# A fused four-layer network on one core: the mixture layer's loads and shared expert rearranged, and softmax sums inverted as rows in two of its attentions

## The chip, the core and the metric

The program runs as one launch on 1 core of one Trainium2 chip. The metric is the device time of that launch in microseconds (us). TensorE multiplies matrices; VectorE (DVE), ScalarE (ACT) and GpSimd (POOL) work on elements; SyncE (SP) issues most DMAs.

## What is computed

Four layers are applied to `x` (32 sequences of 56 tokens, 128 features). Each adds a gated attention over a context of 1500 keys per sequence, and then a gated feed-forward part. Cut to what matters here:

```python
# layer 1 and layer 3 attention (16 heads of 8 features; layer 3 adds -1e6 * mask, and biases)
attn = softmax(einsum('bqhd,bkhd->bhqk', q, k) * scale, axis=-1)
out = einsum('bhqk,bkhd->bqhd', attn, v).reshape(B, T_q, 128)
return out @ w_o.T

# layer 1 feed-forward: one shared expert, 8 experts, each token goes to its best two
def _swiglu(x, gate_up, down):
    g, u = split(einsum('bsd,fd->bsf', x, gate_up), 2, axis=-1)   # 938 hidden
    return einsum('bsi,di->bsd', silu(g) * u, down)
out = _swiglu(x, shared_gate_up, shared_down)
for e in range(8):
    out = out + cw[..., e:e + 1] * _swiglu(x, experts_gate_up[e], experts_down[e])
```

Layers 0 (masked attention) and 2 (cosine attention and a small mixture) are not touched by the change.

## The kernel before, in words

The parts run one after the other, each in a block of its own that ends with a barrier of all engines: attention 0, feed-forward 0, attention 1, mixture layer 1 (`sort_tokens`, then `ffn1`), attention 2, feed-forward 2, attention 3, feed-forward 3, with a `norm` ahead of each.

**`turned_attention`** is attention 1 ("plain") and attention 3 ("add", with a mask). The outer loop goes over the 32 sequences n, the inner over the 8 head pairs p. TensorE's order is written out by hand: for each p `score` half 0, `turn` third 0, `score` half 1, `turn` third 1, `side_work`, `turn` third 2. `score` makes 112 x 750 logits in PSUM, DVE's `shifted` copies them and takes the maxima, DVE or ACT subtracts these (`lower`), `turn` transposes them two pairs later, ACT's `exp` takes them out, and `weigh` (p = 6, 7 and, of the next sequence, 2, 3) multiplies by the values. `side_work` is: the keys of sequence n + 2 (p = 0 to 2), its values (p = 3 to 5), and the end of sequence n - 1 (p = 6 and 7). All side work shares one PSUM tile, `side`.

The end of a sequence is a chain over three engines. ACT's `mix` copies the weighted values to `mixed` (p = 4). At p = 6 TensorE's `sums` multiplies them by `tile_sum`, a 128 x 128 matrix, so that each of 128 rows holds the softmax sum of its head; DVE's `invert` takes the reciprocal of 128 x 224 numbers. At p = 7 DVE's `normalise` multiplies, TensorE's `out` (4 matmuls with the output matrix) waits for it, and ACT's `finish` copies the result out when p = 0 of the next sequence begins.

**Mixture layer.** `sort_tokens` routes the tokens and ranks them on DVE; its SP stream loads constants and the shared expert, writes zeros to `slots_in` in nine DMAs, and then issues the loads of the eight experts, an `up` (944 KB) and a `down` (472 KB, on 118 partitions) for each. `ffn1` then scatters each token's row to its two slots with 32 indirect DMAs on POOL, while TensorE runs the shared expert on 16 tiles of 112 tokens, each in two halves (8 matmuls of 112 columns up, 4 matmuls down); after it 35 blocks of 128 slots run through their experts in the same two halves, and POOL gathers the results. `up` of one half runs ahead of `down` of the half before; ACT's silu and DVE's multiply stand between them. The blocks need the sorted rows and all experts; SP loads the rows only when the scatters have landed.

Each f32 matmul shows as two passes in the trace, each with its own weight load; a transpose shows as one.

## Time and profile before

| | |
|---|---|
| median of 3 runs | 6507.41 us (6505.57 to 6512.12) |
| profiled execution, device time | 6505.09 us |
| its span, first to last instruction | 6503.3 us |
| TensorE busy | 5399.5 us (83%) |
| DVE busy | 4556.5 us (70%) |
| ACT busy | 3155.4 us (49%) |
| POOL busy | 1967.3 us (30%) |
| mean granted TensorE clock | 0.915 of full |
| attention 1 | about 1700 to 2847 us of the span |
| sort and mixture layer 1 | 2863 to 3319 us |
| attention 3 | about 5280 to 6388 us |

The span is the profiled execution's; 1.8 us of the device time lie outside it. The parts follow one another, so a stage's own end is what counts, and busy shares are only an average of stages with different limits.

### The profile page before, as it was taken

To read this page: it belongs to the slowest core of one execution; us is meant where nothing else is said; L and a number is where in the kernel's file an instruction comes from. 1 tells how busy PE (TensorE), PEld (TensorE's weight loads), DVE (VectorE), ACT (ScalarE), POOL (GpSimd) and SP (SyncE) were. 2 spreads that over 40 slices of the span, in tenths; PEclk is the share of its full clock that TensorE was granted. 3 is DMA by queue.
4 is the path that set the end of the run, shared out by engine and by line. 5 is a ranking of instruction groups with operands and counts; after the bars stand their busy time and mean duration, and the time that the engine had idled before them with its cause. 6 is when DMAs were issued, how large, how long until landed. Compare 5 with 4: busy or idle time off the path is not lost. (4 is left out here: it accounts for less than half of the span.)

```text
span 6503.3 us, 132525 instructions
## 1 busy us (share of the span) xinstructions
PE 5399.5 (83%) x51199; PEld 3938.7 (61%) x51199; DVE 4556.5 (70%) x9168; ACT 3155.4 (49%) x5932; POOL 1967.3 (30%) x1458
## 2 busy tenths in 40 slices
PE   2898898896599999955947999999999658888887
PEld 1777777775277777745933444444444437777775
DVE  6888888885177777751446777777777448778774
ACT  0666666664165555531224444444444225555552
POOL 4766766761122222201011111111110023333330
PEclk6999999998699999977978999999999769999998
DMA  4555555552366666631010000000000068888870
GB/s 109 124 121 125 122 121 125 122 120 54 75 120 131 133 129 126 132 87 50 23 27 25 15 19 14 14 19 14 14 19 4 5 128 148 143 150 150 146 138 10
DMA packets 368260, 544.58 MB, mean 84 GB/s; under 512 B 115654, under 2 KB 247880, under 8 KB 367390
## 3 DMA queue, kind: packets, MB, share of 16 engines
q1 hardware_dynamic: 365678, 533.44, 39.8%
q8 instruction: 378, 6.19, 0.5%
q0 software_dynamic: 2048, 3.67, 0.2%
q14 instruction: 156, 1.28, 0.1%
HBM read 413.08 MB, written 123.90 MB: 83 GB/s over the span
## 5 line engine op out<-in xcount | busy, mean ns | idle before, releaser
L635 DVE CUSTOM_DVE_ANT_0 attn_logits<-attn_scores,attn_shift 112x750 f32<-112x750 f32 x1024 | 943.5, 931 | 468.4 <-PE attn_scores L452 467.7
L555 ACT ACTIVATE attn_probs_t<-attn_pt 125x448 f32<-125x448 f32 x1536 | 831.2, 542 | 780.4 <-PE attn_pt L467 760.3
L467 PEld LDWEIGHTS attn_pt<-ident,attn_logits 112*125 112x125 f32 x6144 | 867.0, 191 | 222.3 <-issue 80.7
L467 PE MATMUL attn_pt<-ident,attn_logits 112*125 112x112 f32 x6144 | 926.2, 274 | 67.8 <-DVE attn_logits L649 42.1
L2241 PE MATMUL attn2k_pk<-attn_wk,attn2k_cn_t 128*125 128x512 f32 x1536 | 737.9, 602 | 39.5 <-ACT attn2k_cn_t L2312 36.7
L2252 PE MATMUL attn2k_pg<-attn2k_kn,attn2k_cn 125*128 125x512 f32 x1536 | 725.0, 594 | 4.5 <-ACT attn2k_gram L2320 2.3
L2407 DVE TENSOR_REDUCE attn2k_ss<-attn2k_sq 125x16 f32<-125x1024 f32 x384 | 467.0, 1216 | 255.4 <-ACT attn2k_sq L2349 255.3
L389 POOL CAST attn_k_parts<-xn_t 128x500 bf16<-128x500 f32 x192 | 199.4, 1039 | 1407.4 <-DVE xn_t L605 1407.3
L1141 ACT ACTIVATE attn_probs_t<-attn_pt 125x448 f32<-125x448 f32 x768 | 414.8, 540 | 308.5 <-PE attn_pt L1029 305.9
L2349 ACT ACTIVATE attn2k_sq<-attn2k_pk 125x1024 f32<-125x1024 f32 x384 | 391.9, 1021 | 326.3 <-PE attn2k_pk L2241 326.2
L452 PE MATMUL attn_scores<-attn_k_packed,attn_q_blocks 96*112 96x375 bf16 x2048 | 523.3, 338 | 24.6 <-POOL attn_q_blocks L379 17.9
L2241 PEld LDWEIGHTS attn2k_pk<-attn_wk,attn2k_cn_t 128*125 128x125 f32 x1536 | 274.1, 187 | 399.3 <-issue 296.9
L1017 PE MATMUL attn_scores<-attn_k_packed,attn_q_blocks 96*112 96x375 bf16 x1024 | 357.2, 349 | 149.3 <-DVE attn_tops L1310 149.3
L2419 DVE TENSOR_TENSOR attn2k_kn<-attn2k_pk,attn2k_rn 125x1024 f32<-125x1024 f32 x384 | 470.1, 1224 | 13.3
L2252 PEld LDWEIGHTS attn2k_pg<-attn2k_kn,attn2k_cn 125*128 125x128 f32 x1536 | 264.1, 192 | 298.2 <-issue 286.3
L1310 DVE CUSTOM_DVE_ANT_0 attn_logits<-attn_scores,attn_bias,attn_floor 112x750 f32<-112x750 f32 x342 | 337.9, 988 | 101.8 <-PE attn_scores L1019 100.2
L649 DVE TENSOR_SCALAR attn_logits<-attn_logits,attn_neg_top 112x1500 f32<-112x1500 f32 x320 | 375.5, 1173 | 0.1
L480 PE MATMUL attn_po<-attn_probs_t,attn_v 125*32 125x112 f32 x12288 | 371.7, 272 | 1.3 <-ACT attn_probs_t L555 1.3
L1130 ACT ACTIVATE attn_logits<-attn_logits,attn_neg_top 112x750 f32<-112x750 f32 x342 | 312.9, 916 | 113.7 <-DVE attn_neg_top L1318 111.6
L2223 POOL COPY attn2k_q_now<-attn_q_t 128x448 f32 (+1 forms) x32 | 17.8, 558 | 1135.4 <-PE attn2k_pz L2273 1135.4
L546 ACT ACTIVATE attn_logits<-attn_logits,attn_neg_top 112x750 f32<-112x750 f32 x384 | 351.2, 915 | 10.5 <-DVE attn_neg_top L643 8.8
L421 PE MATMUL attn_side<-attn_ctx_t,attn_wk 128*128 128x500 f32 x384 | 219.7, 655 | 152.8 <-DVE xn_t L605 86.1
(360 smaller groups left out, 10814.0 us busy)
## 6 DMA issues: line engine op xcount, KB each, us to landing
attn_k_packed<-k_scratch SPq DMA_DIRECT2D x384, 375.0 KB, 5.9
attn_k_packed<-k_scratch SPq DMA_DIRECT2D x384, 187.5 KB, 3.9
k_scratch<-attn_k_parts SPq DMA_DIRECT2D x64, 1125.0 KB, 7.4
attn_ctx_t<-in_ctx_t SPq DMA_DIRECT2D x64, 750.0 KB, 7.3
k_scratch<-attn_k_parts SPq DMA_DIRECT2D x96, 375.0 KB, 4.5
attn_ctx_t<-in_ctx_t SPq DMA_DIRECT2D x96, 250.0 KB, 4.6
attn2k_ctx<-in_ctx SPq DMA_DIRECT2D x32, 750.0 KB
attn_mask_in<-in_mask SPq DMA_DIRECT2D x192, 109.4 KB
```

The costliest lines, as they stand in the source:

```text
L452: last = pe.matmul(scores[h][0:PAIR, b, 0:QTR], q_blocks[:, n % 2, p, :, :].rearrange("p a s -> p (a s)"), k_packed[:, n % 2, p, h * HALF ...
L467: last = pe.transpose(pt[(3 * at + t) % 2][0:KC, (c % 4) * PAIR:(c % 4 + 1) * PAIR], logits[:, at % 3, c * KC:(c + 1) * KC], g.ident[0:PAI ...
L480: last = pe.matmul(po[32 * j:32 * j + 32, grp * PAIR:(grp + 1) * PAIR], v[:, n % 3, c, V1 * p:V1 * p + 32], probs_t[0:KC, grp, c, j * PAIR ...
L555: act.activation(probs_t[0:KC, p // 4, 4 * t:4 * t + 4, (p % 4) * PAIR:(p % 4 + 1) * PAIR], pt[(3 * at + t) % 2][0:KC, 0:QUAD].rearrange(" ...
L635: dve.tensor_tensor_reduce(out=logits[:, at % 3, cols].rearrange("p (b k) -> p b k", b=2), in0=scores[h][0:PAIR, :, 0:QTR], in1=shift[:, n ...
L649: dve.tensor_scalar(at, at, neg_top[:, n % 2, p:p + 1], None, ALU.add).then_inc(dve_lowered, 1)
L1141: act.activation(probs_t[0:KC, at % PV_RING, 4 * t:4 * t + 4, :], pt[(3 * at + t) % 2][0:KC, 0:QUAD].rearrange("p (c q) -> p c q", c=4), A ...
L2241: last = pe.matmul(pk[c % 2][0:KC, b, :], cn_t[:, c % 2, :], wk[:, b * HW:(b + 1) * HW], start=True, stop=True)
L2252: last = pe.matmul(pg[:, b, :], cn[:, j, c, :], kn[:, c % 2, b * HW:(b + 1) * HW], start=(c == 0), stop=(c == CH - 1))
L2349: act.activation(sq[:, c % 2, :].rearrange("p (a b) -> p a b", a=2), pk[c % 2][0:KC, :, :], ACT.Square).then_inc(sq_ready, 1)
L2407: dve.tensor_reduce(ss[:, c % 2, :], sq[:, c % 2, :].rearrange("p (h d) -> p h d", h=H2), AX.X, ALU.add).then_inc(ss_ready, 1)
L2419: dve.tensor_tensor(kn[:, c % 2, :].rearrange("p (h d) -> p h d", h=H2), pk[c % 2][0:KC, :, :].rearrange("p a (h d) -> p (a h) d", h=8), r ...
```

## The change

Attentions 1 and 3: `sums` makes the sums with `mixed` as the stationary operand, 112 rows by 8 head pairs, in two matmuls of 4 columns; `invert` takes the reciprocal of 112 x 8 numbers; a new `widen` on TensorE spreads them to 128 x 224 in `side` with eight matmuls of 32 weight columns and 112 moving columns; `normalise` reads `side`. `widen` takes the place of `out` at p = 7, and `out` goes to p = 0 of the next sequence, between `turn` 0 and `score` 1; `finish` follows the first `exp` of that p. `sums` waits for the `finish` of one sequence earlier than before.

Mixture layer: the down matrices are padded to 128 partitions (512 KB each); the expert loads leave the block of the sort and go to the head of `ffn1`'s SP stream; POOL, no longer the sort's SP stream, waits for the zeros. The shared expert runs on 4 quads of 448 tokens in 8 parts (2 matmuls of 448 columns up, 4 matmuls of 128 columns down into one PSUM bank), ACT copies a quad in one instruction. The blocks compute as before.

```diff
                 def sums(n):
                     pe.wait_ge(mixed_ready, n + 1)
                     pe.wait_ge(v_ready, 3 * min(n + 4, B))
-                    wait(pe, y_copied, n)
-                    pe.matmul(side[:, 0:2 * PAIR], tile_sum[:], mixed[:], start=True, stop=True).then_inc(sums_ready, 1)
+                    wait(pe, y_copied, n - 1)
+                    for grp in range(2):
+                        last = pe.matmul(side[0:PAIR, 4 * grp:4 * grp + 4], mixed[:, grp * PAIR:(grp + 1) * PAIR],
+                                         tile_sum[:, 0:128:32], start=True, stop=True)
+                    last.then_inc(sums_ready, 1)
+
+                def widen(n):
+
+                    pe.wait_ge(inv_ready, n + 1)
+                    for p in range(HP):
+                        last = pe.matmul(side[32 * (p % 4):32 * (p % 4) + 32, (p // 4) * PAIR:(p // 4 + 1) * PAIR],
+                                         inv[:, p:p + 1].broadcast_to((PAIR, 32)), g.ident[0:PAIR, 0:PAIR],
+                                         start=True, stop=True)
+                    last.then_inc(inv_wide, 1)
...
-                        sums(n - 1) if p == 6 else out(n - 1)
+                        sums(n - 1) if p == 6 else widen(n - 1)
...
                         if some:
                             turn(*before, 0)
+                        if p == 0 and n > 1:
+                            out(n - 2)
                         score(n, p, 1)
...
+                out(B - 2)
                 sums(B - 1)
+                widen(B - 1)
                 out(B - 1)
...
-                        if p == 0 and n > 1:
-                            finish(n - 2)
                         for t in range(3):
                             if before[0] >= 0:
                                 exp(*before, t)
+                            if p == 0 and t == 0 and n > 1:
+                                finish(n - 2)
...
-                finish(B - 2)
                 for p in (HP - 2, HP - 1):
                     for t in range(3):
                         exp(B - 1, p, t)
+                finish(B - 2)
                 mix(B - 1)
...
                 def invert(n):
                     dve.wait_ge(sums_ready, n + 1)
-                    dve.reciprocal(inv[:], side[:, 0:2 * PAIR]).then_inc(inv_ready, 1)
+                    wait(dve, inv_wide, n)
+                    dve.reciprocal(inv[:], side[0:PAIR, 0:HP]).then_inc(inv_ready, 1)
 
                 def normalise(n):
-                    dve.wait_ge(inv_ready, n + 1)
+                    dve.wait_ge(inv_wide, n + 1)
                     wait(dve, y_ready, n)
-                    dve.tensor_tensor(attn[:], mixed[:], inv[:], ALU.mult).then_inc(attn_ready, 1)
+                    dve.tensor_tensor(attn[:], mixed[:], side[:, 0:2 * PAIR], ALU.mult).then_inc(attn_ready, 1)
...
-                for e in range(E):
-                    sp.dma_start(o.up[:, e, :], a["experts_up_t"][e]).then_inc(o.experts_in, 16)
-                    sp.dma_start(o.down[:, e, :, :], a["experts_down_t"][e]).then_inc(o.experts_in, 16)
-                sp.wait_ge(o.slots_zeroed, 16 * ((NB + 3) // 4))
...
-        o.up, o.down = r.sb("up", [D, E + 1, 2 * FULL1]), r.sb("down", [F1C, E + 1, F1K, D])
+        o.up, o.down = r.sb("up", [D, E + 1, 2 * FULL1]), r.sb("down", [128, E + 1, F1K, D])
...
-        half = TILES
-        units = [("tile", t) for t in range(half)] + [("block", b) for b in range(NB)] + \
-            [("tile", t) for t in range(half, TILES)]
-        N = 2 * len(units)
+        units = [("quad", q) for q in range(NQ)] + [("block", b) for b in range(NB)]
+        parts = {"quad": F1K, "block": 2}
+        items = [(u, j) for u, (kind, n) in enumerate(units) for j in range(parts[kind])]
+        N = len(items)
...
+                for e in range(E):
+                    sp.dma_start(o.up[:, e, :], a["experts_up_t"][e]).then_inc(o.experts_in, 16)
+                    sp.dma_start(o.down[:, e, :, :], a["experts_down_t"][e]).then_inc(o.experts_in, 16)
                 load(0)
                 load(1)
...
             @block.gpsimd
             def _(pool):
+                pool.wait_ge(o.slots_zeroed, 16 * quads)
                 for t in range(TILES):
...
+                    if kind == "quad":
+                        wait(pe, h_ready, i - 1)
+                        for bank, at in ((pg, j * F1C), (pu, FULL1 + j * F1C)):
+                            last = pe.matmul(bank[i % 2][0:F1C, 0:QUAD], o.up[:, E, at:at + F1C],
+                                             g.xn_t[:, n * QUAD:(n + 1) * QUAD], start=True, stop=True)
+                        last.then_inc(up_ready, 1)
+                        return
...
+                        if kind == "quad":
+                            last = pe.matmul(py[u % 2][0:PAIR, k * D:(k + 1) * D], h[:, i % 2, k * PAIR:(k + 1) * PAIR],
+                                             o.down[0:F1C, E, j, :], start=(j == 0 and k == 0),
+                                             stop=(j == F1K - 1 and k == 3))
...
-    return np.ascontiguousarray(out.reshape(F1K, F1C, D).transpose(1, 0, 2))
+    return np.pad(out.reshape(F1K, F1C, D).transpose(1, 0, 2), ((0, 128 - F1C), (0, 0), (0, 0)))
```

## Rows read from the trace of the kernel before

**Rows 1.** Busy time by stretch: start:end, length, engines, PEclk, DMA share, GB/s.
```profile
2000.00:2400.00 400.00, 362.38 (x4323) 309.86 (x4323) 303.34 (x637) 235.00 (x421) 99.10 (x84) 0.96 0.69 131
5400.00:6500.00 1100.00, 931.98 (x10904) 780.64 (x10904) 819.83 (x1614) 583.86 (x1044) 353.52 (x218) 0.97 0.70 126
```

**Rows 2.** Order of time, TensorE, attention 1: start, us, what [idle before].
```profile
2102.89 0.56 PE L436 MATMUL attn_side<-attn_mixed,attn_tile_sum 128*128 128x224 f32 x2
2103.29 0.59 PE L467 MATMUL attn_pt<-ident,attn_logits 112*125 112x112 f32 x4
...
2106.21 0.59 PE L467 MATMUL attn_pt<-ident,attn_logits 112*125 112x112 f32 x4
2108.01 1.10 PE L441 MATMUL attn_side<-attn_attn,attn_wo 128*128 128x56 f32 x8 [1.21 <-DVE attn_attn L658]
2108.94 1.02 PE L467 MATMUL attn_pt<-ident,attn_logits 112*125 112x112 f32 x4
2109.89 2.47 PE L480 MATMUL attn_po<-attn_probs_t,attn_v 125*32 125x112 f32 x48
```

**Rows 3.** Order of time, TensorE, the same place in attention 3.
```profile
5904.47 1.10 PE L441 MATMUL attn_side<-attn_attn,attn_wo 128*128 128x56 f32 x8 [1.21 <-DVE attn_attn L658]
...
5905.98 1.36 PE L480 MATMUL attn_po<-attn_probs_t,attn_v 125*32 125x112 f32 x48
```

**Rows 4.** Order of time, DVE: the reciprocal, once a sequence, attentions 1 and 3.
```profile
2038.47 1.55 DVE L653 RECIPROCAL attn_inv<-attn_side 128x224 f32<-128x224 f32 x1
...
2072.17 1.55 DVE L653 RECIPROCAL attn_inv<-attn_side 128x224 f32<-128x224 f32 x1
...
2104.36 1.55 DVE L653 RECIPROCAL attn_inv<-attn_side 128x224 f32<-128x224 f32 x1
...
5866.80 1.54 DVE L653 RECIPROCAL attn_inv<-attn_side 128x224 f32<-128x224 f32 x1
...
5900.82 1.55 DVE L653 RECIPROCAL attn_inv<-attn_side 128x224 f32<-128x224 f32 x1
```

**Rows 5.** Order of time: a spread like the new one, a small reciprocal, ACT's finish.
```profile
678.14 0.92 PE L988 MATMUL attn_po<-ident,attn_share 112*32 112x112 f32 x16
...
2856.99 0.25 DVE L204 RECIPROCAL norm_rs<-norm_sd 112x16 f32<-112x16 f32 x1 [0.28 <-ACT norm_sd L215]
...
5906.53 0.30 ACT L566 ACTIVATE y_t<-attn_side,attn_bo 128x56 f32<-128x56 f32 x1
```

**Rows 6.** Order of time: the sort's last on DVE, then ffn1's first, and POOL's scatters.
```profile
2887.45 0.17 DVE L1863 TENSOR_SCALAR ffn_expert<-sort_expert 1x35 int32<-1x35 f32 x1
...
2961.78 0.71 PE L1972 MATMUL ffn_pg<-xn_t,ffn_up 128*118 128x112 f32 x2 [80.36 <-PEq L105]
...
2962.53 1.19 POOL L1927 DMA_INDIRECT slots_in<-rows,ffn_slot  x1 [98.74 <-POOLq L105]
...
3001.40 0.94 POOL L1927 DMA_INDIRECT slots_in<-rows,ffn_slot  x1 [0.30 <-issue]
```

**Rows 7.** SP's last expert load, and two 2 us stretches: clock, DMA share, GB/s.
```profile
2958.26 2.53 SPq L1778 DMA_DIRECT2D ffn_down<-in_experts_down_t  x1
...
2914.00:2916.00 2.00, 0.50 0.13 52
2936.00:2938.00 2.00, 0.50 0.97 373
```

**Rows 8.** Order of time, ACT and TensorE, during the scatters of ffn1.
```profile
3006.90 0.55 ACT L2026 ACTIVATE ffn_silu<-ffn_pg 118x448 f32<-118x448 f32 x1 [32.42 <-DMA q_scratch<-attn_probs_t]
...
3008.15 2.05 PE L1986 MATMUL ffn_py<-ffn_down,ffn_h 118*112 118x128 f32 x8 [19.12 <-DVE ffn_h L2047]
```

**Rows 9.** Order of time, TensorE: first block's transposes; a 500-column matmul and its successor.
```profile
3079.87 0.60 PE L1946 MATMUL ffn_pt<-ident,ffn_rows_in 128*128 128x128 f32 x4
...
2113.90 1.02 PE L421 MATMUL attn_side<-attn_ctx_t,attn_wk 128*128 128x500 f32 x2
2114.76 0.59 PE L467 MATMUL attn_pt<-ident,attn_logits 112*125 112x112 f32 x4
```

More of the change, by code:

```diff
@@ L1751, in sort_tokens @@
         ends, reached, expert = r.sb("ends", [1, E]), r.sb("reached", [1, NB, E]), r.sb("expert", [1, NB])
-        zeros = r.sb("zeros", [128, 4, D])
         pl = r.ps("pl", [128, TILES, E])
@@ L1918, in _ @@
                         load(b // 4 + 2)
-                    sp.wait_ge(taken, half + b + 1)
+                    sp.wait_ge(taken, NQ + b + 1)
                     sp.dma_start(slots_out[b * BLK:(b + 1) * BLK, :], rows_out[:, b % 4, :]).then_inc(
@@ L1970, in up @@
                         for bank, at in ((pg, 0), (pu, FULL1)):
-                            at += (4 * part + k) * F1C
-                            last = pe.matmul(bank[i % 2][0:F1C, k * w:(k + 1) * w], w_up[:, at:at + F1C], src,
+                            at += (4 * j + k) * F1C
+                            last = pe.matmul(bank[i % 2][0:F1C, k * BLK:(k + 1) * BLK], up_now[:, n % 2, at:at + F1C],
+                                             rows_t[:, n // 4 % 2, n % 4 * BLK:(n % 4 + 1) * BLK],
                                              start=True, stop=True)
@@ L2006, in take @@
                     kind, n = units[u]
-                    act.wait_ge(down_ready, 2 * u + 2)
-                    if kind == "tile":
-                        to = total[:, n, :]
+                    act.wait_ge(down_ready, done(u))
+                    if kind == "quad":
+                        act.activation(total[:, 4 * n:4 * n + 4, :].rearrange("p t d -> p (t d)"), py[u % 2][0:PAIR, :],
+                                       ACT.Copy).then_inc(taken, 1)
                     else:
                         wait(act, block_out[n % 4], 16 * (n // 4))
-                        to = rows_out[:, n % 4, :]
-                    act.activation(to, py[u % 2][0:width(u), 0:D], ACT.Copy).then_inc(taken, 1)
-                for i in range(N):
-                    u, part = divmod(i, 2)
+                        act.activation(rows_out[:, n % 4, :], py[u % 2][:, 0:D], ACT.Copy).then_inc(taken, 1)
+                for i, (u, j) in enumerate(items):
                     kind, n = units[u]
-                    if kind == "block" and part == 0:
+                    cols = cols_of(u)
+                    if kind == "block" and j == 0:
                         if n == 0:
@@ L2026, in _ @@
                     act.activation(silu[:, i % 2, 0:cols], pg[i % 2][0:F1C, 0:cols], ACT.Silu).then_inc(silu_ready, 1)
-                    if part == 1 and u:
+                    if j == 1 and u:
                         take(u - 1)
@@ L2039, in choose @@
                         :, bass.ds(e * (2 * FULL1), 2 * FULL1)]).then_inc(chosen_up, 1)
-                for i in range(N):
-                    cols = 4 * width(i // 2)
-                    if i == 2 * half:
+                for i, (u, j) in enumerate(items):
+                    kind, n = units[u]
+                    cols = cols_of(u)
+                    if u == NQ and j == 0:
                         choose(0)
@@ L2048, in _ @@
                                       ALU.mult).then_inc(h_ready, 1)
-                    if i % 2 == 0 and half <= i // 2 < half + NB - 1:
-                        choose(i // 2 - half + 1)
+                    if kind == "block" and j == 0 and n + 1 < NB:
+                        choose(n + 1)
                 dve.wait_ge(taken, len(units))
```

58 lines of the change are left out of this document (26 added, 32 removed).

## Prediction

> **What bounds the kernel now.** The parts run one after the other, so I read first the busy time by stretch, then, stage by stage, the instructions in order of time, and asked what each engine waits for at the place of the change. In the two attentions TensorE is busy 91% and 85% of the time, DVE 75%, ACT 59% and 53% [rows 1]. TensorE's order is written out by hand, so every bubble in it is paid in full, and there is one bubble per sequence at the change: `out` comes 1.21 us after the end of the `turn` before it and waits for `normalise` on DVE [rows 2, 3]. That chain is late because the reciprocal takes 1.55 us of DVE [rows 4]. In attention 1 the same place holds a second loss. The `turn` behind `out` takes 1.02 us instead of 0.59, and the `weigh` after it 2.47 instead of 1.36 [rows 2, 3]: TensorE's granted clock has fallen from 2.4 to 1.2 GHz right after the bubble. The distance from one reciprocal to the next shows this loss whole. It is 32.19 us from 2072.17 to 2104.36 and 33.70 us before [rows 4]; of the 28 distances in attention 1 ahead of the last two, 21 are the long ones. In attention 3 the plain distance is 34.02 us [rows 4] and only 2 of 27 are longer, by 1.6 us.
>
> In the mixture layer the sort's own work ends at 2887.45 + 0.17 us, but `ffn1` starts at 2961.78, and TensorE and POOL both stand idle until then [rows 6]. The block of the sort is held open by SP, which issues its last expert load at 2958.26 for 2.53 us [rows 7]: the issues are held back by the loads ahead of them. After that the shared expert is disturbed while POOL scatters: ACT starts a silu 32.42 us after its last work, TensorE then waits 19.12 us for the result of it, and both go on at 3007 to 3008, 4.6 us after POOL's last scatter ended (3001.40 + 0.94) [rows 6, 8]. From 3008.15 to the first block at 3079.87 TensorE runs without a gap [rows 8, 9], and so it does through the blocks, which compute as before.
>
> **The change, part 1: attentions 1 and 3.** For one sequence, on TensorE:
> - `sums` before: 0.40 us (2102.89 to 2103.29) [rows 2]. After: four passes that each load 112 weight columns for 4 moving columns. Nearest row: `out`, eight passes bound by their weight loads, takes 0.93 us from its start to the next (2108.01 to 2108.94) [rows 2], so 0.116 a pass, 0.46 us in all. It costs 0.06.
> - `widen`, new: sixteen passes of 32 weight columns by 112. The same form in attention 0 took 0.92 us [rows 5]; `weigh`, with the same shape in the same four column groups, takes 1.36 for 48 passes [rows 3], so 0.45 for 16. I take 0.45, since `weigh` runs at this very place; 0.92 is the upper end.
> - The bubble goes. In issue time it is 1.80 (2106.21 to 2108.01) less the 0.42 that a `turn` takes, 1.38 us [rows 2]. `normalise` is still wanted by `out`, but `out` now comes after a `turn`, a `weigh`, a `score` and another `turn`, some 2.5 us after `widen`. On DVE the reciprocal falls from 1.55 us to about 0.25, the row for 112 x 16 [rows 4, 5], so `invert` is done before `widen` asks, and `normalise` needs no wait beyond the second `shifted` of p = 7. `normalise` reads PSUM now; even 0.3 us more is hidden in those 2.5.
> - `out` keeps its price and its engine; only its place moves.
> Sum: 0.06 + 0.45 - 1.38 = -0.87 us, for 31 sequences in each attention (at p = 7 for n from 1, the last one in the tail): 62 x 0.87 = 54 us. Ends: with 0.92 for `widen`, 25 us; with 0.45 and a shorter DVE chain at p = 0 of the next sequence, 60.
>
> What is late next: `keys` at p = 0 waits for `finish`, which now stands behind an `exp` on ACT and behind `out`. From the end of `out` TensorE has a `score` and a `turn`, 0.75 us, before `keys`; `finish` takes 0.30 [rows 5] plus about 0.2 to be released on either side. It fits, by a little. The `turn` of pair 6 at p = 0 needs ACT's second `lower`, which is not later than now, because `negate` at p = 6 comes 1.3 us sooner.
>
> The clock: with the bubble gone, the longest waits left near this place are under half of it, while waits of about 0.6 us at the keys in p = 1 to 3 are not followed by slow matmuls. I expect the long distances to vanish: 21 x 1.51 = 32 us in attention 1, 2 x 1.6 = 3 in attention 3, 35 in all. The other end is 0.
>
> The tails: `out` of sequence 30 and its `finish` now stand ahead of the last `mix` on ACT, about 1.3 us, `widen` and one more hand-over cost 0.7, the reciprocal gives back 1.3. Twice +0.7: +1.
>
> Attentions: -54 - 35 + 1 = -88 us.
>
> **Part 2: the expert loads leave the sort.** The sort ends with DVE at 2887.62 instead of with SP at 2960.79 (2958.26 + 2.53) [rows 6, 7]: -73.2 us for the start of `ffn1`, with what the next block needs to begin unchanged. SP carries nothing else that late: the zeros are issued before the experts, and POOL now waits for them, behind which only the scatters stand. The cost of the move is that the loads now run beside the scatters and the shared expert. SP's row loads stand behind sixteen load issues, so the loads must be through before the first block. The down loads on 118 partitions moved 52 GB/s at a DMA share of 0.13, the up loads 373 GB/s at 0.97 [rows 7]. Eight experts are 8 x (944 + 512) KB = 11.9 MB; at 250 to 370 GB/s that is 32 to 48 us, so they end at about 2921 to 2937. At 118 partitions a pair took 12.3 us (one issue of each kind together) and the whole would end near 2987. The first block is due at about 3007 (below): even that is hidden, and the 128 partitions alone give nothing on the path.
>
> The disturbance during the scatters: 32 scatters at 1.25 us [rows 6] now run from about 2889.4 to 2929.2. I carry over what the trace shows, ACT and TensorE resuming 4.6 to 5.8 us after the last scatter's end: TensorE at 2935. From there it needs 71.7 us (3008.15 to 3079.87) [rows 8, 9] less part 3, so the first block is at 3007 - 3 = 3004, against 3079.87: -76 us with part 3. Ends: the disturbance gone, -100 (3008.15 - 2972 of waiting falls away for the most part); lengthened by the loads, -55.
>
> **Part 3: quads.** The same columns, longer matmuls. A matmul of 500 columns takes 0.86 us (2113.90 to 2114.76) [rows 9], so 448 take 0.77 and two 1.54, against 1.65 for eight of 112 columns (71.7 us over 28 halves, less 0.87 for the down part and the slow first ones). 0.11 x 28 = 3 us, bounded by 0 and 5. ACT's silu and DVE's multiply, 1.2 us together, stand beside 2.4 us of TensorE work.
>
> DMA rule weighed: the two-engine rate above is in line with the Trainium skill, "DMA: Bandwidth & Descriptors", section on why a DMA increments its semaphore by 16, and changes no number. Against the change speaks the same page's section on queues, rings and completion order: each DMA engine takes the queues in turn, a packet at a time. By it the scatters would wait for expert packets until the loads are through. The trace has no scatter beside a full load; by this rule the disturbance would end later than by my sum (rival D).
>
> **Rivals.**
> A, the forecast: 6507.4 - 88 - 76 = 6343. For the profiled execution 6505.1 - 164 = 6341; it stands 2.3 us under the median of the runs, and I count from the median. Ranges of its own: 6330 to 6356. 50%.
> B, the clock still falls after some weak stretch of attention 1 (`sums` and `out` move few columns): +35, 6378. For it: 21 of 28 sequences fall now. Against it: where the waits are 0.6 us it does not fall. 14%.
> C, the disturbance is a lack of instructions, and quads have half of them: the wait to 3008 shrinks, up to 30 us: 6313. For it: nothing that ACT or TensorE needs in those 32 us is late by the program's own order, and the page lists a DMA as releaser that has nothing to do with it. Against it: ACT has as many instructions as before up to that silu. The Trainium skill, "Runtime: NRT & Kernel Launch", section on instruction fetch, has engines refill their instructions by DMA in blocks; by that rule halving them would help; no row here shows such a transfer in those 32 us. 14%.
> D, the scatters are slowed by the expert loads, say to the 2937 at which these end plus half of the scatters (20 us): the resumption at 2957 instead of 2935: 6365. Against it: at 2962 to 2970 scatters ran beside the last down load at their usual pace. 17%.
> E, slower than before: under the loads TensorE crawls through all of the shared expert. Between 2961.78 and 3008.15 it got 5 of the 32 halves done, 9.3 us each [rows 6, 8]. All 32 at that pace are 297 us, against 118 before (2961.78 to 3079.87): +179 on the forecast, 6522. It decides once 24 more halves crawl (164 us at 9.3 less 2.5 each), that is, if loads and scatters held on past 3150; they carry under 50 us of data. 2%.
> F, the attention part does not do what it says: `keys` waits for `finish` as long as `out` waited for `normalise`. The 54 us go, the clock loss stays: 6343 + 89 = 6432. 3%.
>
> **How the numbers follow.** The likeliest is A, 6343. B and D above, C below give 6313 to 6378; with the ends of `widen` (+29) and of part 2 the range is 6303 to 6390, and leaves out E, F and the corners. Under 0.2%, some 13 us, this kernel's measurement can't tell from no change; all cases but E lie far beyond. Faster 0.97, same 0.01, slower 0.02.
>
> **What would show it.** The distance between two reciprocals about 31.3 us in attention 1 and 33.1 in attention 3, all alike; the reciprocal at 0.2 to 0.3 us; sixteen `widen` passes in 0.45; no wait of TensorE ahead of `out`. `ffn1`'s first matmul at 73 us after where it would have been; expert loads at a DMA share near 1 throughout; the first block's transposes some 76 us sooner in relation to the end of attention 1. The prediction is wrong if `keys` at p = 0 waits over 0.3 us, if matmuls of twice the length stay in attention 1, or if TensorE resumes later than 8 us after the last scatter.

## The result and the profile after

| | before | changed |
|---|---|---|
| median | 6509.76 us (6505.57 to 6512.35, 4 runs) | 6368.2 us (6366.15 to 6371.75, 4 runs) |
| ratio, 95% interval | 1 | 0.9781 (0.9768 to 0.9794) |
| span of the profiled execution | 6503.3 us | 6364.4 us |

The span is 138.9 us shorter. The forecast was 164 us less (6343 us, 6303 to 6390). I cut both traces at the starts of a few instructions: the first and last reciprocal of attention 1, the weight load of the first block's first transpose in the mixture layer (0.1 us ahead of the transpose itself), the first and last small reciprocal of attention 2 (`attn2k_rn`), the first and last reciprocal of attention 3. The table is worked out from those starts.

| stretch | before | changed | difference | forecast |
|---|---|---|---|---|
| attention 1 | 1004.3 | 945.2 | -59.1 | -27 - 32 = -59 |
| last reciprocal to first block | 236.4 | 150.0 | -86.4 | -76 |
| attention 2 | 1557.5 | 1576.2 | +18.7 | 0 |
| attention 3 | 1029.6 | 1022.1 | -7.5 | -27 - 3 = -30 |
| all the rest | 2675.5 | 2670.9 | -4.6 | +1 |

So 59 us came as worked out, 10 more than expected came in the mixture layer, and two stretches ate 41: attention 3 kept little of its gain, and attention 2, whose code isn't touched, became slower.

Changed kernel, the page: span, busy times, the queue that carries instructions of all engines but TensorE (packets, MB, share).

```profile
span 6364.4 us, 134097 instructions
PE 5422.2 (85%) x51967; PEld 3936.1 (62%) x51967; DVE 4490.0 (71%) x9168; ACT 3160.1 (50%) x5920; POOL 1966.7 (31%) x1458
q14 instruction: 222, 1.82, 0.1%
```

Before, TensorE was busy 5399.5 us; it is busy 22.7 us longer now, so what went is waiting.

Changed kernel, TensorE in order of time, attention 1, the place of [rows 2].

```profile
2118.95 0.47 PE L439 MATMUL attn_side<-attn_tile_sum,attn_mixed 128*112 128x4 f32 x4
2119.28 0.67 PE L481 MATMUL attn_pt<-ident,attn_logits 112*125 112x112 f32 x4
...
2122.80 0.59 PE L447 MATMUL attn_side<-ident,attn_inv 112*32 112x112 f32 x16
2123.32 0.69 PE L481 MATMUL attn_pt<-ident,attn_logits 112*125 112x112 f32 x4
2123.93 1.36 PE L494 MATMUL attn_po<-attn_probs_t,attn_v 125*32 125x112 f32 x48
...
2126.01 1.01 PE L455 MATMUL attn_side<-attn_attn,attn_wo 128*128 128x56 f32 x8
2126.86 0.49 PE L466 MATMUL attn_scores<-attn_k_packed,attn_q_blocks 96*112 96x375 bf16 x2
```

`sums` (L439) takes 0.33 us from its start to the next, where 0.46 was estimated; `widen` (L447) 0.52, estimated 0.45; `out` (L455) has no wait in brackets; the `turn` and the `weigh` behind it are 0.69 and 1.36 long instead of 1.02 and 2.47. The reciprocal, the same kernel on DVE, against 1.55 us in [rows 4]:

```profile
2120.41 0.21 DVE L672 RECIPROCAL attn_inv<-attn_side 112x8 f32<-112x8 f32 x1
...
2151.77 0.21 DVE L672 RECIPROCAL attn_inv<-attn_side 112x8 f32<-112x8 f32 x1
```

The distance is 31.36 us, and the 28 distances of attention 1 all lie between 31.36 and 31.50.

Attention 3, one sequence of the changed kernel in order of time: TensorE, then DVE, then POOL.

```profile
5829.39 1.05 PE L429 MATMUL attn_side<-attn_wv,attn_ctx_t 128*125 128x128 f32 x8
...
5832.54 0.69 PE L481 MATMUL attn_pt<-ident,attn_logits 112*125 112x112 f32 x4 [1.34 <-DVE attn_logits L667]
...
5834.45 1.94 PE L429 MATMUL attn_side<-attn_wv,attn_ctx_t 128*125 128x128 f32 x8
5836.18 1.02 PE L481 MATMUL attn_pt<-ident,attn_logits 112*125 112x112 f32 x4
...
5829.65 2.84 DVE L667 TENSOR_SCALAR attn_logits<-attn_logits,attn_neg_top 112x1500 f32<-112x1500 f32 x1
...
5827.69 4.00 POOL L374 TENSOR_SCALAR attn_shift<-attn_shift 112x1500 f32<-112x1500 f32 x1
```

To be read from below: POOL scales the mask of the next sequence (L374); DVE's `lower` beside it takes 2.84 us, where it takes 0.99 otherwise, and ends 0.8 us after POOL does (5832.49 against 5831.69); TensorE waits 1.34 us for it; and then the values' matmuls (L429) take 1.94 us instead of 1.05 and a `turn` 1.02 instead of 0.59. The kernel before has the same wait at this place, but no long matmuls behind it:

```profile
5860.30 0.69 PE L467 MATMUL attn_pt<-ident,attn_logits 112*125 112x112 f32 x4 [1.34 <-DVE attn_logits L649]
...
5861.94 1.05 PE L428 MATMUL attn_side<-attn_wv,attn_ctx_t 128*125 128x128 f32 x8
```

So 25 of the 28 distances ahead of the last three are 34.2 to 34.5 us, where the forecast was 33.1; the other three are 33.0 to 33.1. Added up, these 28 take 956.8 us, and 955.7 before: the sequences gained nothing, and what attention 3 gained came in its last three distances (73.9 us before, 65.3 now).

Mixture layer of the changed kernel: TensorE, ACT, POOL in order of time, against [rows 6, 8, 9].

```profile
2827.95 1.81 PE L1975 MATMUL ffn_pg<-xn_t,ffn_up 128*118 128x448 f32 x2 [7.18 <-PEq L105]
2846.88 1.77 PE L2005 MATMUL ffn_py<-ffn_down,ffn_h 118*112 118x128 f32 x8 [3.40 <-issue]
2870.71 2.05 PE L2005 MATMUL ffn_py<-ffn_down,ffn_h 118*112 118x128 f32 x8 [19.51 <-issue]
...
2933.13 0.60 PE L1966 MATMUL ffn_pt<-ident,ffn_rows_in 128*128 128x128 f32 x4
...
2869.46 0.54 ACT L2049 ACTIVATE ffn_silu<-ffn_pg 118x448 f32<-118x448 f32 x1 [23.29 <-DMA q_scratch<-attn_probs_t]
...
2867.64 0.94 POOL L1947 DMA_INDIRECT slots_in<-rows,ffn_slot  x1 [0.30 <-issue]
```

The 80.36 us of idle ahead of the first matmul are 7.18 now. The disturbance is still there: TensorE goes on 2.1 us after the end of the last scatter (5.8 before).

### The profile page after: what moved, and what is told of

It is laid out like the page before. It is cut to its first block and busy times, and to the rows that moved or that the text cites. A ratio compares the mean times of both kernels' runs of the same rounds, so it can differ in the third digit from the quotient of the medians.

```text
span 6364.4 us, 134097 instructions
## 1 busy us (share of the span) xinstructions
PE 5422.2 (85%) x51967; PEld 3936.1 (62%) x51967; DVE 4490.0 (71%) x9168; ACT 3160.1 (50%) x5920; POOL 1966.7 (31%) x1458
## 3 DMA queue, kind: packets, MB, share of 16 engines
q8 instruction: 384, 6.29, 0.5%
## 5 line engine op out<-in xcount | busy, mean ns | idle before, releaser
L2443 DVE TENSOR_TENSOR attn2k_kn<-attn2k_pk,attn2k_rn 125x1024 f32<-125x1024 f32 x384 | 470.2, 1224 | 13.3
L494 PE MATMUL attn_po<-attn_probs_t,attn_v 125*32 125x112 f32 x12288 | 347.3, 261 | 1.3 <-ACT attn_probs_t L573 1.3
```

The source lines that it names most:

```text
L2443: dve.tensor_tensor(kn[:, c % 2, :].rearrange("p (h d) -> p h d", h=H2), pk[c % 2][0:KC, :, :].rearrange("p a (h d) -> p (a h) d", h=8), r ...
```

## The experiments

The experiments ran in four comparisons on four chips, which the record numbers. Beside them the kernel before took 6474 us on chip 12, 6512 on chip 8, 6471 on chip 6 and 6509 on chip 13; in the first comparison, whose chip has no number on record, it took 6510. By these times I call 8, 13 and the first comparison's the slower chips, 6 and 12 the faster ones. Whole times are compared within a comparison only; the stretches, apart from the mixture layer's, agree across chips within 1 to 3 us. All ratios are against the kernel before beside it.

| kernel | chip | median us | ratio (interval) | attention 1 | to first block | attention 2 | attention 3 |
|---|---|---|---|---|---|---|---|
| no_wait | 12 | 6321.5 | 0.9763 (0.9747 to 0.9779) | 945.7 | 122.8 | 1557.6 | 1021.8 |
| mask_act | 12 | 6248.9 | 0.9650 (0.9634 to 0.9666) | 945.4 | 121.3 | 1557.6 | 945.6 |
| att_only | 12 | 6422.7 | 0.9916 (0.9899 to 0.9933) | 946.0 | 201.9 | 1577.0 | 1026.4 |
| mix_only | 12 | 6392.1 | 0.9870 (0.9853 to 0.9886) | 1006.2 | 123.3 | 1557.6 | 1031.3 |
| changed | 8 | 6369.5 | 0.9782 (0.9765 to 0.9798) | 944.7 | 153.7 | 1575.6 | 1020.9 |
| out_moved | 8 | 6308.7 | 0.9683 (0.9666 to 0.9700) | 928.0 | 153.0 | 1559.0 | 990.5 |
| out_at_once | 8 | 6395.0 | 0.9823 (0.9807 to 0.9840) | 977.0 | 154.2 | 1557.5 | 1033.8 |
| down118 | 8 | 6356.2 | 0.9763 (0.9747 to 0.9780) | 945.1 | 152.8 | 1557.6 | 1021.8 |
| both | 6 | 6230.1 | 0.9626 (0.9610 to 0.9642) | 927.9 | 123.5 | 1557.3 | 953.1 |
| sort_loads | 6 | 6232.3 | 0.9633 (0.9617 to 0.9649) | 928.1 | 126.5 | 1557.3 | 943.3 |
| late_scatters | 6 | 6230.6 | 0.9622 (0.9606 to 0.9638) | 926.9 | 123.2 | 1557.3 | 949.5 |
| shifted_late | 13 | 6278.5 | 0.9643 (0.9627 to 0.9659) | 927.7 | 154.0 | 1575.3 | 948.3 |

### Attention 2: where a loop lies in DVE's program

**no_wait** takes one line out of the changed kernel:

```diff
                 def invert(n):
                     dve.wait_ge(sums_ready, n + 1)
-                    wait(dve, inv_wide, n)
                     dve.reciprocal(inv[:], side[0:PAIR, 0:HP]).then_inc(inv_ready, 1)
```

> The changed kernel without the new wait of invert for inv_wide (normalise of the sequence before, on the same engine, has waited for it already); nothing else. DVE's program is 62 instructions shorter by it, 31 of them ahead of the loop of attention 2, and as long as in the kernel before. Theory (attention 2 lost its time because the added instructions shifted its loop in DVE's instruction stream): the stretch from the mixture layer's first block transposes to attention 3's first reciprocal goes back from 2292.0 to about 2275 us, the instruction packets on DVE's queue in attention 2 from 60 to a handful, the time from 6368 to 6351 us. Rival (attention 2 lost it by something else, such as where its data lie or what the mixture layer leaves running): no change, 6368 us.

The stretch is back at 1557.6 us. Attention 2, both kernels over the same 1400 us: first changed (instruction packets; DVE in order of time in an iteration), then no_wait.

```profile
q14 instruction: 68, 0.56, 0.1%
...
4005.18 1.22 DVE L2431 TENSOR_REDUCE attn2k_ss<-attn2k_sq 125x16 f32<-125x1024 f32 x1 [2.08 <-ACT attn2k_sq L2373]
4007.49 0.87 DVE L2400 BATCH_NORM_STATS2 attn2k_stats<-attn2k_ctx 125x6 f32<-125x128 f32 x4 [1.09 <-issue]
```

```profile
q14 instruction: 4, 0.03, 0.0%
```

Attention 2 is a loop on every engine, 14 iterations of two sequences. In the changed kernel DVE stands before L2400 once an iteration, 13 times, 14.5 us in all, and 64 packets of 8 KB more are fetched, five an iteration. The expected time, 6351, missed: this run was beside a before of 6474, where 6321.5 is a ratio of 0.9763. Beside the changed kernel on chip 8, down118 (no_wait but for a load that proves hidden) took 13.3 us less, and its attention 2 18.0. A rule of the Trainium skill bears on this: "Runtime: NRT & Kernel Launch", section on instruction fetch mechanics, says that a taken branch whose target has left the two held blocks forces a fetch. The trace agrees that a branch can cost a fetch each time; the packets on this queue are 8 KB, not the 16 KiB that the page gives (those on TensorE's queue are 16 KB: 384, 6.29 MB). What no page and no view tells is which position is the bad one.

**shifted_late** puts the same number of DVE instructions back by other means. It stands on late_scatters (below).

```diff
+                for _ in range(61):
+                    dve.wait_ge(o.shared_in, 32)
                 for i, (u, j) in enumerate(items):
```

> late_scatters with 61 more waits on DVE at the head of ffn1, all on a semaphore that has long been there (they make DVE's program 31 instructions longer ahead of attention 2, as the wait in invert did in attention 1). Theory (attention 2 loses its 17 to 19 us by where its loop lies in DVE's program): attention 2's first to last reciprocal takes 1576 us again instead of 1557, and the time is 17 to 20 us over late_scatters. Rival (the wait in invert slowed attention 2 in some other way): 1557 us. On a chip with the disturbance (before at 6512) also what late_scatters expected of it: if the scatters hold up the shared expert, its gap comes 40 to 66 us behind ffn1's first matmul; if not, at 18 to 43.

1575.3 us, and 221 packets on this queue in the whole program, against 1557.3 and 156 in late_scatters. The two kernels differ in these waits alone, long satisfied and in another stage (they ran on chips 13 and 6, but attention 2 takes 1557 to 1559 us on either kind of chip without the added instructions). So it is the position of the loop, and the wait in `invert` slowed nothing where it stands. Only these two positions, 31 instructions apart, were tried. att_only (31 instructions more ahead of the loop) and mix_only (none) say the same.

### The two parts alone

**att_only** is the kernel before with the diff's hunks in `turned_attention`, **mix_only** with those of the mixture layer.

> The kernel before with only the attention part of the change. If the two parts are independent: attention 1 -59 us, attention 3 -7.5, attention 2 +17 by DVE's shifted instructions, so about 6509.8 - 50 = 6460 us; the stretch of attention 2 as slow as in the changed kernel. Rival (the slower attention 2 comes from the mixture layer's part): 6443 us, with attention 2 as fast as before.

> The kernel before with only the mixture layer's part of the change. Independent parts: -86 us between the last out of attention 1 and the first block, nothing elsewhere: 6424 us, attention 2 as fast as before (DVE's program is as long as before). Rival (the disturbance of the shared expert or attention 2 depend on the attention part, or the mixture part brings the loss of 17): 6441 us.

-51.1 and -81.7 us beside a before of 6473.8. The ratios multiply to 0.9787, the whole change has 0.9781: the parts are independent. The absolute times expected missed, since they were worked out from 6510 and the runs were on a faster chip.

### Attention 3: the mask on POOL

**mask_act** is no_wait with

```diff
                 def push(n):
                     pool.wait_ge(mask_in[n % 2], (n // 2 + 1) * 32)
                     pool.tensor_scalar(shift[:, n % 2, :], shift[:, n % 2, :], -1000000.0, None,
-                                       ALU.mult).then_inc(push_ready, 1)
+                                       ALU.mult).then_inc(push_ready, 2)
...
-                    if add and 0 < n < B - 1:
-                        push(n + 1)
...
+                def push(n, h):
+                    act.wait_ge(mask_in[n % 2], (n // 2 + 1) * 32)
+                    at = shift[:, n % 2, h * HALF:(h + 1) * HALF]
+                    act.activation(at, at, ACT.Copy, scale=-1000000.0).then_inc(push_ready, 1)
...
+                            if add and p == 6 and t < 2 and 0 < n < B - 1:
+                                push(n + 1, t)
...
-                            dve.wait_ge(push_ready, n + 1)
+                            dve.wait_ge(push_ready, 2 * (n + 1))
```

> no_wait with one more edit in attention 3: the mask is scaled on ACT in two halves at p = 6, and no longer on POOL at p = 4. Theory (while POOL scales the mask, DVE's lower of p = 3 takes 2.84 us instead of 0.99, TensorE waits 1.34 us for it, and its clock then falls, which takes the rest of what the attention part should have gained in attention 3): the wait and the long matmuls go, the distance between reciprocals in attention 3 falls from 34.27 to 31.6 to 33.0 us, which is 35 to 75 us less than no_wait. Rival (the clock falls in attention 3 because sums, widen and out are a weak stretch of TensorE): the distance falls by the 1.34 us wait at most, to 32.9, or not at all, and matmuls of twice the length stay.

72.6 us less than no_wait beside it, 76.2 of them in attention 3; the distance is 31.4 us there, as in attention 1. DVE's `lower` by line over 5500 to 6100 us (count, busy, mean ns) and the stretch itself (TensorE's busy time first, the clock third from the end), changed and then mask_act:

```profile
L667 DVE TENSOR_SCALAR attn_logits<-attn_logits,attn_neg_top 112x1500 f32<-112x1500 f32 x88 | 118.6, 1348 | 0.0
...
5500.00:6100.00 600.00, 545.29 (x6660) 466.23 (x6660) 459.07 (x932) 348.44 (x618) 224.64 (x142) 0.96 0.82 147
```

```profile
L672 DVE TENSOR_SCALAR attn_logits<-attn_logits,attn_neg_top 112x1500 f32<-112x1500 f32 x98 | 97.6, 996 | 0.0
...
5500.00:6100.00 600.00, 564.87 (x7255) 482.78 (x7254) 463.30 (x1019) 399.50 (x713) 150.24 (x127) 1.00 0.87 154
```

The slow `lower`s are gone (all are 1.0 us), the wait is gone, and the granted clock is 1.00. So the falls needed that wait, and `sums`, `widen` and `out`, which move few columns, don't bring them by themselves; the rival is out. The wait alone isn't enough either. Four kernels have it in each of the 28 sequences ahead of the last three, and the granted clock fell behind it in 25 sequences of the changed kernel, in 10 of out_moved, in 2 of out_at_once (both below) and in none of the kernel before (clock 0.99 over the same 600 us). The last two are those in which TensorE also waits ahead of `out`, 0.51 and 1.21 us.

### Attention 1: rows, or the place of `out`?

**out_moved** is no_wait with the old sums and no `widen`:

```diff
-                    for grp in range(2):
-                        last = pe.matmul(side[0:PAIR, 4 * grp:4 * grp + 4], mixed[:, grp * PAIR:(grp + 1) * PAIR],
-                                         tile_sum[:, 0:128:32], start=True, stop=True)
-                    last.then_inc(sums_ready, 1)
+                    pe.matmul(side[:, 0:2 * PAIR], tile_sum[:], mixed[:], start=True, stop=True).then_inc(sums_ready, 1)
...
-                    elif n > 0:
-                        sums(n - 1) if p == 6 else widen(n - 1)
+                    elif n > 0 and p == 6:
+                        sums(n - 1)
...
-                    dve.reciprocal(inv[:], side[0:PAIR, 0:HP]).then_inc(inv_ready, 1)
+                    dve.reciprocal(inv[:], side[:, 0:2 * PAIR]).then_inc(inv_ready, 1)
...
-                    dve.wait_ge(inv_wide, n + 1)
+                    dve.wait_ge(inv_ready, n + 1)
...
-                    dve.tensor_tensor(attn[:], mixed[:], side[:, 0:2 * PAIR], ALU.mult).then_inc(attn_ready, 1)
+                    dve.tensor_tensor(attn[:], mixed[:], inv[:], ALU.mult).then_inc(attn_ready, 1)
```

> no_wait with the softmax sums as in the kernel before (one matmul with tile_sum, a reciprocal of 128 x 224, no widen), but with out and finish where the change has put them. Theory (the gain comes from the new place of out; the rows only pay for widen): the reciprocal takes 1.55 us again and nobody on TensorE waits for it, the distance in attention 1 is 31.36 less 0.51 = 30.9 us, the time 62 x 0.51 = 32 us under no_wait. Rival (the long reciprocal holds up DVE's negate of p = 6 and with it ACT's lower, the turn of p = 6 and the shifted of p = 7): a new wait of up to 1.3 us, distance 31.4 to 32.2, the time 0 to 50 us over no_wait.

60.8 us faster than the changed kernel beside it, 47.5 faster than down118, which has the new sums. TensorE at the place of [rows 2]:

```profile
2124.85 0.59 PE L468 MATMUL attn_pt<-ident,attn_logits 112*125 112x112 f32 x4
2125.28 1.01 PE L442 MATMUL attn_side<-attn_attn,attn_wo 128*128 128x56 f32 x8
```

No wait ahead of `out`, though the reciprocal takes 1.55 us again; the distance is 30.8 us. So once `out` has moved, the rows bring nothing and cost `widen`. In attention 3 out_moved gains 31.3 us over down118, twice what `widen` explains: the mean clock over 5500 to 6100 us is 0.98 there instead of 0.95, and the clock falls in 10 sequences instead of 25.

**out_at_once** is no_wait with `out` right behind `widen` at p = 7:

```diff
+                    elif n > 0 and p == 6:
+                        sums(n - 1)
                     elif n > 0:
-                        sums(n - 1) if p == 6 else widen(n - 1)
+                        widen(n - 1)
+                        out(n - 1)
...
-                        if p == 0 and n > 1:
-                            out(n - 2)
```

> no_wait with out right behind widen at p = 7, so the sums inverted in rows and the old place of out. Theory (moving out is what removes the wait; the short reciprocal alone leaves the hand-over to normalise and back): out waits 0.7 to 1.0 us, the distance in attention 1 is 32.1 to 32.4, and where TensorE's clock falls behind that wait as it did in the kernel before, 33.7; the time is 50 to 130 us over no_wait. Rival (the short reciprocal was enough): out waits under 0.3 us and the time is that of no_wait.

```profile
2128.88 0.59 PE L447 MATMUL attn_side<-ident,attn_inv 112*32 112x112 f32 x16
2129.98 1.10 PE L455 MATMUL attn_side<-attn_attn,attn_wo 128*128 128x56 f32 x8 [0.51 <-DVE attn_attn L676]
2130.91 0.65 PE L481 MATMUL attn_pt<-ident,attn_logits 112*125 112x112 f32 x4
2131.49 1.36 PE L494 MATMUL attn_po<-attn_probs_t,attn_v 125*32 125x112 f32 x48
```

The wait is 0.51 us, shorter than I expected, and the distance 32.4, as expected, because `keys` now waits 0.3 us for `finish` as well. It is 38.8 us slower than down118, under the 50 that I gave. The `turn` and `weigh` behind the wait have full speed in every sequence: a wait of 0.51 us was not followed by a slower clock, the 1.21 us of before was, in 21 of 28 in attention 1 (in attention 3 only in 2 of 28). In attention 3 the distance is 34.26 us, the same as with `out` moved (34.27 in the changed kernel): there the clock's falls took back all that the new place of `out` gave a sequence.

### The mixture layer

**changed** is the changed kernel once more.

> The changed kernel once more, on the chip of these runs. In the first comparison its shared expert was disturbed (27 us between ffn1's first matmul and the first block more than the 78 that no_wait took); att_only, mix_only and no_wait showed no disturbance, and the kernel before was some 36 us faster beside them. Theory (the disturbance belongs to the chip and not to the code): on a chip where the kernel before takes about 6474 us the changed kernel has no disturbance, its first block stands 123 us behind attention 1's last reciprocal, and it takes about 6338 us, 17 more than no_wait; where before takes 6510, 150 us and 6368. Rival (the removed wait, or the shift of DVE's instructions, removed the disturbance): 150 us and some 6366 beside a before of 6474.

On chip 8, a slower one, 153.7 us to the first block where 150 was said; all four kernels of that comparison have 152.8 to 154.2, and the six on chips 6 and 12 that have the mixture layer's part 121 to 127. The same 8 us (clock, DMA share, GB/s at the end), changed and then no_wait:

```profile
2852.00:2860.00 8.00, 1.63 (x3) 0.32 (x1) 0.00 (x0) 0.00 (x0) 6.17 (x7) 0.71 1.02 419
```

```profile
2852.00:2860.00 8.00, 8.00 (x46) 5.64 (x45) 1.98 (x4) 2.66 (x5) 6.16 (x7) 1.00 1.02 418
```

The same scatters, the same DMA load, and TensorE is mostly idle on one and full on the other. The rival is out: down118 has the wait removed too, and the disturbance with it on chip 8. So the disturbance goes with the chip and not with these edits. The changed kernel itself was not run on a faster chip, so its 6338 us there stay untested.

**down118** is no_wait with the down matrices loaded on 118 partitions, `o.down[0:F1C, e, :, :]`.

> no_wait with the experts' down matrices loaded on 118 partitions instead of 128, at the new place. By the rows of before a pair of up and down then takes 12.3 us, the eight 98 us from ffn1's start, where the 128 partitions took some 32. By the prediction's step this is hidden where the shared expert is disturbed (first block 105 us behind ffn1's first matmul). Where it isn't, the first block is due at 78 us and waits some 20 to 25 us for the last expert: 20 to 25 us over no_wait. Rival (the rest of the queue, rows and results, doesn't care): no difference; other rival (up and down loads overlap, 9.1 us each pair, 73 us in all): no difference either.

SP's last expert load, down118 and then the changed kernel:

```profile
2906.06 1.76 SPq L1931 DMA_DIRECT2D ffn_down<-in_experts_down_t  x1
```

```profile
2841.06 1.86 SPq L1932 DMA_DIRECT2D ffn_down<-in_experts_down_t  x1
```

65 us later, and the first block at the same place (152.8 us). The DMA share fell to 0.5 during the scatters and the disturbance stayed, so it doesn't come from the expert loads filling the DMA engines. On a faster chip, where the block is due 30 us sooner, this wasn't run.

**sort_loads** is both (next section) with the 16 issues back in the sort's stream.

> both with the expert loads back in the SP stream of the sort, behind the zeros, on 128 partitions. Theory (the end of the sort is the last issue of a load, which the loads ahead of it hold back): 11.9 MB at some 400 GB/s are 30 us from the zeros' end at about 2800 on this kernel's clock, less than what the sort needs on DVE (to some 15 to 20 us behind that): ffn1 starts 5 to 20 us later than in both, not 73; so of the 73 us most come from the 128 partitions and the move brings 5 to 20. Rival (the move alone brings the 73 us, the width nothing): ffn1 starts 60 to 75 us later than in both.

The first matmul of `ffn1`, sort_loads and then both:

```profile
2816.79 1.82 PE L1965 MATMUL ffn_pg<-xn_t,ffn_up 128*118 128x448 f32 x2 [10.50 <-PEq L105]
```

```profile
2810.08 1.81 PE L1965 MATMUL ffn_pg<-xn_t,ffn_up 128*118 128x448 f32 x2 [7.17 <-PEq L105]
```

3.3 us more idle, and the time within 2.2 us of both. The padding alone takes away 70 of the 73 us, where 53 to 68 were expected, and by down118 the move alone takes them all away.

**late_scatters** is both with `pool.wait_ge(up_ready, 10)` ahead of the scatters.

> both with POOL waiting, ahead of its first scatter, until TensorE has done ten of the shared expert's 32 up parts (some 24 us). On a chip with the disturbance (before at 6512): if the scatters hold up the shared expert, TensorE runs without a gap until some 15 us behind the first scatter, that is to 40 us behind ffn1's first matmul, and then waits until the last scatter has landed at 66; the first block is at about 100 to 106 us, as now. Rival (it is the start of ffn1, or the expert loads): the gap stays 18 to 43 us behind ffn1's first matmul, whatever the scatters do. On a chip without it (before at 6474): no gap, the first block at 78 us as in no_wait.

It ran on chip 6 and had no gap. shifted_late has the same wait and ran on chip 13, a slower one. TensorE, then POOL's first and last scatter:

```profile
2870.57 2.05 PE L1996 MATMUL ffn_py<-ffn_down,ffn_h 118*112 118x128 f32 x8 [13.49 <-issue]
2886.04 2.05 PE L1996 MATMUL ffn_py<-ffn_down,ffn_h 118*112 118x128 f32 x8 [11.41 <-DVE ffn_h L2064]
...
2839.66 1.19 POOL L1938 DMA_INDIRECT slots_in<-rows,ffn_slot  x1 [50.43 <-PE ffn_pu L1966]
...
2878.51 0.94 POOL L1938 DMA_INDIRECT slots_in<-rows,ffn_slot  x1 [0.30 <-issue]
```

`ffn1` starts at 2814.07 (changed kernel: 2827.95). TensorE now works through 43 us without a gap, where the changed kernel stops after 16 to 23, and stops 17 us behind the first scatter. At that time the expert loads are over (DMA share 0.17). It goes on 6.6 us after the last. The gap follows the scatters. In the changed kernel the input of ACT's silu at 2869.46 was done at about 2851.2, and DVE and TensorE go on only behind it, so it is ACT that is held up; by what, is open.

### The version that beats both

**both** is out_moved and mask_act together.

> out_moved and mask_act together: no redundant wait, the softmax sums as before with out at its new place, the mask scaled on ACT. Theory (the two gains are independent and both attentions are then alike): the distance between reciprocals is 30.8 us in attention 3 as in attention 1, attention 3's first to last reciprocal 930 us instead of 990.5 in out_moved, the time some 60 us under out_moved: 6248 where the kernel before takes 6512, 6213 where it takes 6474. Rival (in attention 3 ACT has no room for the mask beside the later negate): 0 to 30 us less than out_moved.

0.9626 against 0.9763 for no_wait (chips 6 and 12). It is 17 us slower than expected: attention 1 is at 30.8 us a sequence, attention 3 too, but for a few sequences of up to 39.7, and takes 953 instead of 930 us. TensorE in the worst of them:

```profile
5305.36 0.48 PE L466 MATMUL attn_pt<-ident,attn_logits 112*125 112x112 f32 x3
5311.25 0.55 PE L466 MATMUL attn_pt<-ident,attn_logits 112*125 112x112 f32 x1 [5.42 <-issue]
```

It stops between the third and the fourth pass of one `turn`, with nothing to wait for; the packet on TensorE's instruction queue came at 5307.85, the one before at 5288.26. A late instruction fetch at a DMA share of 1.05 would look like this. That was not tried. All four kernels with the old sums and the mask on ACT have five to seven such stops of over 1 us in attention 3, 11 to 16 us in all, and mask_act, which has `widen`, has none and takes 945.6 us there. So with the mask on ACT the old sums are shown to pay in attention 1 alone, and both isn't clearly faster than mask_act (0.9626 and 0.9650, intervals that overlap).

## Why the prediction was right in sign and 25 us too low

- **The bubble, `sums`, `widen`.** Right: 31.36 us a sequence against 31.3. `sums` was oversized by 0.13 us and `widen` undersized by 0.07. The step "`out` comes after ... some 2.5 us after `widen`" holds (2.7 us from 2123.32 to 2126.01), and so does `keys` without a longer wait (F is out).
- **The clock in attention 1.** Right: 21 slow sequences became none, 32 us. B is out there. Its reason was too coarse: "the longest waits left near this place are under half of it" looks at one place only. (The 28 distances stand ahead of the last three, not the last two, and attention 3 has 28 as well, not 27; no sum changes.)
- **Attention 3.** The step that failed is the sum's 31 x 0.87 + 3 us: 7.5 came, none of it in the first 28 sequences. I listed the waits near the change and not those elsewhere in the sequence. The 1.34 us wait at the mask was in the trace of before; with the old bubble gone the clock falls behind that wait. The three sequences in which it doesn't are at the forecast 33.1 us. mask_act shows that the falls need this wait, and out_at_once that they go nearly all away when a wait of 0.51 us is left ahead of `out`. Why a wait at one place keeps the clock up behind another is open.
- **Attention 2.** The step that failed is that nothing beyond the two parts was counted: the added `wait(dve, inv_wide, n)` was costed at nothing in time, rightly, but not in instructions. 31 instructions ahead of a loop cost 18.7 us, shown by removing them and by adding others.
- **Start of `ffn1`.** Right: from attention 1's last reciprocal 118.5 us (2961.78 - 2843.33) became 44.9 (2827.95 - 2783.01), -73.5 against -73.2. "The 128 partitions alone give nothing on the path" is true beside the move only; each edit alone is enough (sort_loads, down118).
- **Quads.** Right: from `ffn1`'s first matmul to the first block 82.0 us in att_only, 78.2 in no_wait, 3.8 against 3, both on chip 12, without the disturbance.
- **The disturbance.** The term was mis-sized: it was carried over whole. First matmul to first block took 118.1 us before (36.1 more than undisturbed) and 105.2 now (27.0 more), so 9 us less. Of these, 3.6 us are that TensorE goes on 42.8 us after `ffn1`'s first matmul (2870.71 - 2827.95) instead of 46.4; the other 5.5 must be work that it had done before it stopped. The run changed has the same code and kept more of the disturbance: 108.9 us from first matmul to first block, 30.7 more than undisturbed, and TensorE goes on 6.4 us after the last scatter instead of 2.1. So up to 4 of the 9 us need not be an effect of the change. C's explanation isn't shown by this: between 2851 and 2869 us, while ACT stands still, the changed kernel's trace has no packet on either instruction queue. The place of the gap goes with the scatters.
- **Rival D**, scatters slowed by loads, is out. 31 scatter distances took 38.9 us in both kernels (2828.70 to 2867.64), beside a DMA share of 1.0. The Trainium skill's rule ("DMA: Bandwidth & Descriptors", queues, rings and completion order) of packets taken in turn may hold for the packets; POOL's pace doesn't show it, and TensorE went on 2.1 us (in changed 6.4) after the last scatter, so it had no price here that shows beside the 5.8 of before. E is out too.

## What to carry to other kernels

A wait is removed by moving the waiter behind other work before anything is spent on shortening the chain that it waits for: here the shorter chain brought the wait from 1.21 to 0.51 us with `out` at its old place, and with `out` moved it cost `widen` and bought nothing. When a bubble goes, list every wait of the iteration, not those near the edit, since another one can become the one behind which the clock falls. And count instructions as well as time: a free wait ahead of a loop can move the loop to where each iteration fetches its code again, so compare the instruction packets of stages that weren't touched.

## What the runs showed of the hardware

- A loop that lay 31 DVE instructions further on fetched five 8 KB packets more an iteration and took 18.7 us more for its 14 iterations.
- DVE's 112 x 1500 subtraction took 2.84 us beside a POOL operation on 112 x 1500 (4.00 us) and 0.99 without it; ACT did the same scaling in two halves of 0.82 us, and DVE's subtraction stayed at 1.0 us.
- A 1.34 us wait of TensorE was followed by a fall of the granted clock, with matmuls of about twice the length, in 25 of 28 sequences of one kernel, in 10 and in 2 of two others, and in none of a fourth; a wait of 0.51 us was not, in any.
- While 32 scatters of 1.25 us were issued, ACT and TensorE lost 27 to 36 us on the slower chips and nothing on the faster ones (late_scatters and shifted_late differ in 61 waits of DVE alone: 123.2 and 154.0 us to the first block). The kernel before took 6509 to 6512 us on the former and 6471 to 6474 on the latter.
